# Softmax attention in a transformer chain: 64-wide values with two heads side by side, and the output weights applied per pair of heads

## The reference, cut to what matters

```python
D_MODEL, N_HEADS, D_KV = 128, 16, 64
q = shape(hidden_states @ w_q)      # [B, 16 heads, 256, 64]
k = shape(hidden_states @ w_k)
v = shape(hidden_states @ w_v)
scores = jnp.einsum('bhqd,bhkd->bhqk', q, k) + position_bias
attn = jax.nn.softmax(scores, axis=-1)
ctx = jnp.einsum('bhqk,bhkd->bhqd', attn, v)
ctx = jnp.transpose(ctx, (0, 2, 1, 3)).reshape(B, S, 16 * 64)
return ctx @ w_o                    # w_o is [1024, 128]
```

## Time and profile before

| what | value |
|---|---|
| time, median of 3 executions | 2850.93 us (2838.46 to 2852.52) |
| the profiled execution's own time | 2836.4 us |
| its span in the trace | 2834.8 us |
| stretch of the softmax attention's steady groups | about 1600 to 2600 us of the span |
| busy share there, 100 us pieces | TensorE 98 to 99%, VectorE 93 to 95%, ScalarE 88 to 90%, GpSimd 84 to 86% |

### The profile page before, as it was taken

One profiled execution on the slowest core, in us unless ns is written; L12 is line 12 of the kernel. 1 busy time (PEld: TensorE's weight loads), 2 busy tenths in 40 slices (PEclk: granted clock), 3 DMA queues, 4 the chain that ended last, 5 costly groups with the idle time before them and its releaser, 6 DMA issues. The chain is left out here.

```text
span 2834.8 us, 60232 instructions
## 1 busy us (share of the span) xinstructions
PE 2084.8 (74%) x14603; PEld 1528.8 (54%) x14603; DVE 2163.0 (76%) x8149; ACT 1620.7 (57%) x4488; POOL 1744.0 (62%) x2414
## 2 busy tenths in 40 slices
PE   2225878568232688850687799999999999996787
PEld 2225777456221577740455466666666666664565
DVE  4423878788442377776899899999999999997897
ACT  3213444255321344424555688888898888886564
POOL 4554656600455365662465488888888888886565
PEclk9999999889555799985899899999999999998999
DMA  5114333240311433326000276666666666664000
GB/s 172 39 44 116 109 105 113 74 123 0 114 39 50 113 106 104 110 71 187 30 0 0 55 137 138 140 138 142 140 138 137 137 137 139 139 142 104 11 22 27
DMA packets 703407, 272.35 MB, mean 96 GB/s; under 512 B 560020, under 2 KB 688852, under 8 KB 702468
## 3 DMA queue, kind: packets, MB, share of 16 engines
q1 hardware_dynamic: 680628, 229.75, 33.8%
q0 software_dynamic: 17408, 35.82, 3.9%
q10 hardware_dynamic: 5200, 4.84, 0.5%
HBM read 59.31 MB, written 44.24 MB: 37 GB/s over the span
## 5 line engine op out<-in xcount | busy, mean ns | idle before, releaser
L2239 ACT ACTIVATE p_prob<-p_neg,p_neg_max 128x256 f32<-128x256 f32 x1024 | 507.3, 500 | 2.6 <-DVE p_neg_max L2123 2.6
L1044 POOL DMA_INDIRECT results_by_token<-p_e_result,p_e_slot x288 | 284.7, 988 | 249.4 <-DVE p_e_result L987 172.6
L2123 DVE CUSTOM_DVE_ANT_0 p_neg<-p_s_ps,top_bias 128x256 f32<-128x256 f32 x1024 | 381.7, 408 | 1.7 <-PE p_s_ps L2417 1.7
L730 POOL DMA_INDIRECT rows_by_expert<-p_r_z,p_r_target x256 | 247.0, 965 | 201.1 <-issue 111.6
L881 PE MATMUL p_e_o_ps<-p_w,p_e_hT 128*128 x2304 | 297.1, 281 | 15.9 <-issue 14.7
L2134 DVE SCALAR_TENSOR_TENSOR p_parts<-p_prob,p_scaled_inverse,p_parts 128x256 f16<-128x256 f32 x512 | 303.8, 632 | 0.8 <-POOL p_parts L2322 0.8
L918 ACT ACTIVATE p_e_hT<-p_e_h_ps,p_b 128x256 f32<-128x256 f32 x576 | 230.9, 476 | 122.7 <-PE p_e_h_ps L872 78.0
L2338 POOL TENSOR_TENSOR p_parts<-p_prob,p_parts 128x512 f16<-128x512 f32 x256 | 296.5, 1158 | 0.0
L881 PEld LDWEIGHTS p_e_o_ps<-p_w,p_e_hT 128*128 128x128 f32 x2304 | 279.8, 197 | 23.8 <-issue 21.4
L2417 PE MATMUL p_s_ps<-p_qkT 64*128 64x256 f32 x2048 | 290.1, 402 | 2.9 <-ACT p_qkT L2258 2.6
L2372 PE MATMUL p_o_ps<-p_probT,p_val 128*128 128x256 f16 x1024 | 282.8, 276 | 6.7 <-DMA p_probT<-p_parts 6.7
(11 more groups left out here) (280 smaller groups left out, 5672.6 us busy)
## 6 DMA issues: line engine op xcount, KB each, us to landing
p_e_z<-rows_by_expert SPq DMA_DIRECT2D x144, 129.0 KB
p_e_affine<-p_affine SPq DMA_DIRECT2D x144, 128.0 KB
p_got<-results_by_token SPq DMA_DIRECT2D x64, 256.0 KB, 2.8
p_e_b<-p_b SPq DMA_DIRECT2D x144, 64.0 KB
p_probT<-p_parts SPq DMA_TRANSPOSE x512, 2.8
results_by_token<-p_e_result,p_e_slot POOLq DMA_INDIRECT x288
p_r_w<-in_w SPq DMA_DIRECT2D x2, 2048.0 KB, 8.0
p_w<-in_w SPq DMA_DIRECT2D x2, 2048.0 KB, 11.9
```

The lines of the kernel that those rows point to most:

```text
L730: pool.indirect_dma_start(dram_rows, bass.IndirectOffsetOnAxis(ap=target[s][:, r, k:k + 1], axis=0), z[s][:, r, k, :], None).then_inc(scat ...
L1044: pool.indirect_dma_start(dram_results, bass.IndirectOffsetOnAxis(ap=slot[q][:, t:t + 1], axis=0), result[q % 2][:, t, :], None).then_inc( ...
L2123: ins = v.tensor_tensor_reduce(neg[k % NEGS][:, t, :], s_ps[k % SCORES][:, t, :], bias[:, t, h, :], -1.0, HUGE, ALU.add, ALU.min, neg_max[ ...
L2239: ins = act.activation(prob[k % PROBS][:, t, :], neg[k % NEGS][:, t, :], ACT.Exp, bias=neg_max[k % NEGS][:, t:t + 1], scale=-1.0, accum_ou ...
```

## The change

The fold is dropped. Values stay 64 wide: a slot makes two token tiles of four heads (6 matmuls of 128x256), so a quad needs two value slots and not four (j = 2 to `act_ps`, j = 7 to `v_ps`); j = 3 and j = 6 are empty. `outputs` is called once for a pair of units, at odd steps: 12 matmuls, alternately for the first head into PSUM partitions 0 to 63 and for the second into 64 to 127 of `ctx_ps`, one buffer. VectorE copies that context to SBUF at even steps (`keep_context`, L2157 of the new program), and `mix` multiplies the copy by the output weights of the pair, in fp32, adding all pairs up in `o_ps` with tokens on the partitions, so that nothing has to be turned. `keep_output` and `turn_output` are gone; one `add_output` per group. z's turn moves from step 16 to step 21.

```diff
@@ constants @@
-VALUE_SLOTS = (1, 3)
+FIRST_VALUE, SECOND_VALUE = 1, 3
+CONTEXTS = 4
+FIRST_SLOTS, SECOND_SLOTS = (0, 1, 2), (0, 2, 3)
-FIRST_BANK = ((Q, 0), (V, 0), (Q, 1), (V, 2))
-SECOND_BANK = ((K, 0), (V, 1), (K, 1), (V, 3))
+FIRST_BANK = ((Q, 0), (V, 0), (Q, 1), None)
+SECOND_BANK = ((K, 0), None, (K, 1), (V, 1))
@@ buffers @@
-        b_high = m.sb("b_high", [P, HEADS, D], F16)
-        b_low = m.sb("b_low", [P, HEADS, D], F16)
+        wv_high = m.sb("wv_high", [P, HEADS * D_HEAD], F16)
+        wv_low = m.sb("wv_low", [P, HEADS * D_HEAD], F16)
-        val = [m.sb(f"val{b}", [P, 2, GT, QUAD * D], F16) for b in range(2)]
+        val = [m.sb(f"val{b}", [P, 2, GT, QUAD * D_HEAD], F16) for b in range(2)]
-        outT = [m.sb(f"outT{b}", [P, SEQ]) for b in range(GROUP_SEQS)]
+        ctxT = [m.sb(f"ctxT{b}", [P, SEQ]) for b in range(CONTEXTS)]
-        o_ps = [m.ps(f"o_ps{b}", [P, 2, SEQ]) for b in range(GROUP_SEQS)]
+        ctx_ps = m.ps("ctx_ps", [P, SEQ])
+        o_ps = m.ps("o_ps", [P, GT, D])
-        Z_BEHIND, Z_UNIT = (2, 0), 2 * UNITS
+        Z_QUAD, Z_UNIT = 2, 2 * UNITS + 5
@@ SyncE, turn_parts @@
-                    sp.wait_ge(o_read, i * GROUP_UNITS + (k - TURNS + 1))
+                    sp.wait_ge(o_read, i * (GROUP_UNITS // 2) + ((k - TURNS) // 2 + 1))
@@ VectorE @@
-            def add_output(i, b):
-                v.wait_ge(o_turned[b], i + 1)
-                xs = x_res[:, bass.ds(i * GT + b * SEQ_TILES, SEQ_TILES), :]
-                v.tensor_tensor(xs, o_ps[b][:, 1, :].rearrange("p (t d) -> p t d", d=D), xs, ALU.add).then_inc(o_added[b], 1)
+            def add_output(i):
+                v.wait_ge(mixed, pair_number(i, GROUP_UNITS - 2))
+                xs = x_res[:, bass.ds(i * GT, GT), :]
+                v.tensor_tensor(xs, o_ps[:], xs, ALU.add).then_inc(o_added, 1)
+
+            def keep_context(i, k):
+                v.wait_ge(o_read, pair_number(i, k))
+                if not early(i, k, 2 * CONTEXTS):
+                    v.wait_ge(mixed, pair_number(i, k) - CONTEXTS)
+                v.tensor_scalar(ctxT[k // 2 % CONTEXTS][:], ctx_ps[:], OUT_SCALE, None, ALU.mult).then_inc(ctx_kept, 1)
...
-                    if j // 2 in VALUE_SLOTS:
-                        (keep_low_second if j % 2 else keep_low_first)(i, g, j // 2)
-                    elif j % 2 == 0 and has_slot(g, j // 2, ahead):
+                    if j == 2 * FIRST_VALUE:
+                        keep_low_first(i, g)
+                    elif j == 2 * SECOND_VALUE + 1:
+                        keep_low_second(i, g)
+                    elif j % 2 == 0 and has_slot(g, j, ahead):
                         take_queries(*projection(i, g, j // 2))
+                    if j % 2 == 0 and unit_before(i, k, 8):
+                        keep_context(*unit_before(i, k, 8))
@@ TensorE @@
                 if of == V:
-                    toks, heads = slice(n * P, (n + 1) * P), slice(g * QUAD, (g + 1) * QUAD)
-                    return three_passes(out, (src[:, 0, toks], src[:, 1, toks]),
-                                        (b_high[:, heads, :].rearrange("p h d -> p (h d)"), b_low[:, heads, :].rearrange("p h d -> p (h d)")))
+                    wide = QUAD * D_HEAD
+                    cols = slice(g * wide, (g + 1) * wide)
+                    for t in range(SEQ_TILES):
+                        toks = slice((n * SEQ_TILES + t) * P, (n * SEQ_TILES + t + 1) * P)
+                        ins = three_passes(out[:, t * wide:(t + 1) * wide], (src[:, 0, toks], src[:, 1, toks]), (wv_high[:, cols], wv_low[:, cols]))
+                    return ins
@@ TensorE, outputs @@
-                pe.wait_ge(turned[k % TURNS], 16 * turn_use(i, k))
-                cols = slice(hd * D, (hd + 1) * D)
+                if not early(i, k, 2):
+                    pe.wait_ge(ctx_kept, pair_number(i, k) - 1)
+                for h in range(2):
+                    pe.wait_ge(turned[(k + h) % TURNS], 16 * turn_use(i, k + h))
                 for c in range(SEQ_TILES):
-                    r = b * SEQ_TILES + c
-                    ins = three_passes(o_ps[b][:, 0, :].rearrange("p (t q) -> p t q", q=P), (val[g % 2][:, 0, r, cols], val[g % 2][:, 1, r, cols]),
-                                       (probT[k % TURNS][:, 0, :, c, :], probT[k % TURNS][:, 1, :, c, :]),
-                                       start=first and c == 0, stop=last and c == SEQ_TILES - 1)
+                    for of, by in ((HIGH, HIGH), (HIGH, LOW), (LOW, HIGH)):
+                        for h in range(2):
+                            cols = slice((hd + h) * D_HEAD, (hd + h + 1) * D_HEAD)
+                            ins = pe.matmul(ctx_ps[h * D_HEAD:(h + 1) * D_HEAD, :].rearrange("p (t q) -> p t q", q=P),
+                                            val[g % 2][:, of, b * SEQ_TILES + c, cols], probT[(k + h) % TURNS][:, by, :, c, :],
+                                            start=c == 0 and of == by, stop=c == SEQ_TILES - 1 and of == LOW)
                 ins.then_inc(o_read, 1)
+            def mix(i, k):
+                b, pair = k % UNITS // QUAD, quad_of(k) * QUAD_PAIRS + k % QUAD // 2
+                pe.wait_ge(ctx_kept, pair_number(i, k))
+                if k == 0 and not first_group(i):
+                    pe.wait_ge(o_added, i)
+                for t in range(SEQ_TILES):
+                    ins = pe.matmul(o_ps[:, b * SEQ_TILES + t, :], ctxT[k // 2 % CONTEXTS][:, t * P:(t + 1) * P], wo[:, pair, :],
+                                    start=k == 0 and t == 0, stop=pair == SEQ_PAIRS - 1, skip_group_check=True)
+                ins.then_inc(mixed, 1)
@@ TensorE, body @@
-                    before = unit_before(i, k, OUTPUT_LAG)
-                    if before:
-                        outputs(*before)
+                    if k % 2:
+                        if unit_before(i, k, OUTPUT_LAG):
+                            outputs(*unit_before(i, k, OUTPUT_LAG))
+                        for n in {OUTPUT_LAG + 2: (), OUTPUT_LAG + 4: (4, 2)}.get(k, (2,)):
+                            if unit_before(i, k, OUTPUT_LAG + n):
+                                mix(*unit_before(i, k, OUTPUT_LAG + n))
```

More of the change, by code:

```diff
@@ L1937, in bias_attention @@
         exp_ready, inverse_ready = m.sem("exp_ready"), m.sem("inverse_ready")
[L1938 removed]
+        ctx_kept, mixed, o_added = m.sem("ctx_kept"), m.sem("mixed"), m.sem("o_added")
         qk_high, qk_low = m.sem("qk_high"), m.sem("qk_low")
[L1940 removed]
+        wv_half, wv_ready = m.sem("wv_half"), m.sem("wv_ready")
         carried = m.sem("carried")
@@ L2180, in body @@
                         invert(*unit_behind(i, k, 1))
-                    if k == 5 and not first:
-                        add_output(i - 1, 0)
+                    if k == 8 and not first:
+                        add_output(i - 1)
                     if k == 9 and not first:
-                        add_output(i - 1, 1)
-                    if k == 10 and not first:
                         statistics_behind(i - 1)
-            def keep_low_b(n):
-                v.wait_ge(b_high_kept, FOLD_ORDER.index(n) + 1)
-                v.scalar_tensor_tensor(b_low[:, a_heads(n), :], a_bank(n), B_SCALE, b_high[:, a_heads(n), :], ALU.mult, ALU.subtract)\
-                    .then_inc(b_low_kept, 1)
             chain.restart()
@@ L2215, in _ @@
             last = GROUPS - 1
-            for b in range(GROUP_SEQS):
-                add_output(last, b)
+            for k in range(GROUP_UNITS - 8, GROUP_UNITS, 2):
+                keep_context(last, k)
+            add_output(last)
             statistics_behind(last)
@@ L2268, in body @@
                     g, j = quad_of(k), k % UNITS
-                    if j % 2 and has_slot(g, j // 2, ahead):
-                        take_second(*projection(i, g, j // 2))
-                    if j % 2 == 0 and j // 2 in VALUE_SLOTS:
-                        take_high_first(i, g, j // 2)
+                    if j == 2 * FIRST_VALUE:
+                        take_high_first(i, g)
+                    elif j == 2 * SECOND_VALUE + 1:
+                        take_high_second(i, g)
+                    elif j % 2 and has_slot(g, j, ahead):
+                        take_keys(*projection(i, g, j // 2))
                     if k == Z_UNIT + 1 and ahead:
@@ L2279, in body @@
                         high_part(*before)
-                    if k == 3 and not first:
-                        keep_output(i - 1, 0)
-                    if k == 7 and not first:
-                        keep_output(i - 1, 1)
                     if k == Z_UNIT - 5 and ahead:
@@ L2308, in _ @@
                     high_part(last, k)
-            for b in range(GROUP_SEQS):
-                keep_output(last, b)
         @block.gpsimd
@@ L2423, in outputs @@
                 g, b, hd = quad_of(k), k % UNITS // QUAD, k % QUAD
-                first, last = g == 0 and hd == 0, g == QUADS - 1 and hd == QUAD - 1
-                if hd == 0:
```

(20 more changed lines are left out.)

139 lines of the change are left out of this document (58 added, 81 removed).

## The result

The change made the kernel 0.3% slower: 2853.9 us (median of 20) against 2847.07 for the kernel before, measured beside it; ratio 1.0032, 95% interval 1.0016 to 1.0048. The forecast was 0.7% faster. The profiled execution took 2849.2 us (span 2847.4).

What follows compares the result with a forecast made beforehand. TensorE and VectorE were taken to bound the kernel together. VectorE's 58.1 us work plus 3.4 waits gave 61.5 a group, 18 us less over sixteen groups and 1.3 once: 2817 us profiled, 2832 by the median, range 2797 to 2900.

Steps and rivals of the forecast that it cites:

- the step that failed, on the single `ctx_ps`: Outputs wait for the previous pair's copy, ending 1.6 us into VectorE's even step; said to cost nothing, as transposes come later.
- The margin of -0.2 us: Odd unit's transpose against the start of its pair's outputs: a margin of 2.2 us was to become -0.2.
- The list of what is queued behind: TensorE's work behind waiting outputs: slot ready after 2.0 us, needed at 2.6; scores after 3.2, needed at 3.9.
- The rival on them: Late transposes eat the gain: waits 3.1 us or more, group 62.6 us again, no change at 2850 us; chance 25%.
- Waits: VectorE's waits for other engines: forecast 3.4 us a group, against 3.7 before the change.
- The value that I left at 0.06: VectorE's wait at a first value part, put at 0.06 us each, four a group, as before.
- the second value, which I had doubled to 0.65: VectorE's wait at a second value part, doubled from 0.32 to 0.65 us for transposes and mix in the queue.
- VectorE's work: VectorE's work a group: 58.9 us before, +0.6 by count, -1.4 from shorter low parts, forecast 58.1.
- The low part: Probabilities' low part on VectorE: about 1.0 us at j = 1, 3, 5, 7, instead of 1.36 or 0.85.
- TensorE's work: TensorE's work a group: 55.3 us with column halves side by side; 65.8 if one after the other, a rival at 17%.
- It would cost more than 75 us: Clock rival: TensorE idles more and its granted clock drops to 1.2 GHz, costing more than 75 us; chance 3%.
- Vanished waits: Rival: TensorE gets ahead, VectorE alone sets the pace at 58.1 to 60 us a group, 2797 us; chance 8%.

Runs made afterwards that it cites:

- e1: Changed kernel with the context copy ahead of the maxima in VectorE's even step; ratio 0.9967 to the kernel before.
- e9: Changed kernel with the context copies on ScalarE, behind its exponentials in even steps, none on VectorE; ratio 1.0063 to the kernel before.
- e11: Changed kernel with the context copies on ScalarE, ahead of the even step's exponentials, none on VectorE; ratio 0.9938 to the kernel before.
- e4: Changed kernel with outputs, context copy, add and statistics two steps later; ratio 0.9998 to the kernel before.
- e15: Changed kernel with the context copy ahead of VectorE's maxima and outputs two steps later; ratio 0.9730 to the kernel before.
- e17: Changed kernel with TensorE's slot ahead of outputs except at j = 3, outputs two steps later, copies first on ScalarE; ratio 0.9739 to the kernel before.
- e14: Changed kernel with TensorE's slot ahead of outputs except at j = 3, copy first on VectorE, outputs two steps later; ratio 0.9773 to the kernel before.

## Why the prediction was wrong

**"... the transposes come later, so it costs nothing as long as they do."** This is the step that failed, on the single `ctx_ps`. It compared the copy's end with a fixed time of the outputs, 1.6 us into VectorE's even step. The 1.6 us were right: in the timeline of k = 11 the even step's first maximum starts at 2058.29 and the copy ends at 2059.98. But the outputs have no fixed time. TensorE's scores end at 2058.14, before VectorE's even step has begun, and from there TensorE only waits; and what it does behind the held outputs is what VectorE waits for next. At j = 3 nearly all pairs and at j = 1 half of them start within 0.1 us of the copy's end, none at j = 5 and 7. What the step put at nothing measured 93.7 us of TensorE's waits in 10.9 groups, and VectorE waits 5.4 us a group where 3.4 were forecast. e1, e9 and e11 show the cause: moved ahead of its step's other work, the copy is worth 0.64% on VectorE and 1.24% on ScalarE, and with VectorE much less busy but the release late there is a loss.

In groups 3 to 15 the mean is 63.1 where 61.5 was forecast: work 0.2 less, waits 1.9 more, of which the falls of the clock (five of 1.6 us) are 0.6.

**Transposes.** The margin of -0.2 us was right in sign: in e1, where the copy hardly holds the outputs, 58 of some 160 pairs wait for a landing, 0.7 us each. The list of what is queued behind was right too; that VectorE would find the slot and the scores ready (2.0 us against 2.6, 3.2 against 3.9) was not. The rival on them named the right size (waits of 3.1 or more) and missed that they were second: in the changed kernel they are covered by the copy (e4), in e1 they are the bound (e15).

**Waits.** Forecast 3.4 us a group, measured 5.4. The value that I left at 0.06 became 0.39, four a group, 1.3 us; queries 0.8 and scores 1.1 came in that had none; the second value, which I had doubled to 0.65, measured 0.39. They are not separate terms: all are the same held queue.

**VectorE's work.** Forecast 58.1, measured 57.9. The low part came to about 1.0 us as expected, but for j = 7: the medians at j = 1, 3, 5 and 7 were 1.41, 0.87, 1.35 and 0.85 before and are 1.08, 1.02, 1.02 and 0.80 now. At j = 3, from its start to the inverse behind it, it is 1.01 (timeline):

```profile
2060.65 1.09 DVE L2124 SCALAR_TENSOR_TENSOR p_parts<-p_prob,p_scaled_inverse,p_parts 128x256 f16<-128x256 f32 x2
...
2061.66 0.15 DVE L2119 RECIPROCAL p_inverse<-p_total 128x2 f32<-128x2 f32 x1
```

In e17, with no copy on VectorE, it is 1.40 and 1.36 again at j = 1 and 5 (e14: 1.08 and 1.04). That fits the reading that the copy moves it behind GpSimd's subtraction; no run tests the subtraction itself.

**TensorE's work.** The halves do run side by side: the two records of a pair start 3 to 4 ns apart, the next pair 0.109 us later. From start to start, outputs cost 0.776 a pair, mix 0.548, scores 1.067 and a slot 0.745, the pauses in them: 16 x (0.776 + 0.548 + 1.067) + 24 x 0.745 + 0.5 = 56.6, forecast 55.3. The weight loads don't stand bare: a pair's twelve take 0.58 us in all, beside its matmuls. That tiles operate independently (the Trainium skill, TensorEngine Tiling (Array Packing), Key Properties) agrees with these starts.

**The clock.** "It would cost more than 75 us" was put to a fall that lasts. It came in another form, 3.4 us at a time, each group with one 1.6 us longer: 6 of them, some 10 us. I had judged by the earlier trace rows, where TensorE is idle for a sixth of 1420 to 1500 us at a clock of 1.00; in the changed kernel's trace the same 80 us, whose code is not touched, has 0.96, so one window was no evidence.

**Vanished waits.** This rival (8%, 58.1 to 60 us a group) is what e15 and e14 reach, 58.1 and 59.1: the change holds the gain, but its order of work doesn't give it. The sum's parts were thus good for a bound and not for a forecast.

The Trainium skill (Perfetto Trace Analysis, Optimizing Tensor Performance, Matmuls) says that independent groups of matmuls should rotate through PSUM banks, so that emptying one overlaps with the next. The single `ctx_ps` goes against it, and the waits of 93.7 us agree with the rule.
